# Experts' output layer on one Trainium2 core: the activations become the stationary operand

## What the reference computes

```python
h  = gelu(x_e @ W1[e] + b1[e])     # rows x 128 -> rows x 512
ye = h @ W2[e] + b2[e]             # rows x 512 -> rows x 128
out[rows of e] += gate * ye
```

## Time and profile before

| what | value |
|---|---|
| runs of the kernel | 1934.9, 1938.9, 1939.16 us; median 1938.9 us |
| profiled execution | 1937.17 us |
| its span | 1935.3 us |
| TensorE matmul busy | 1583.7 us (82%) |
| TensorE weight loads | 912.9 us (47%) |
| VectorE busy | 1304.5 us (67%) |
| GpSimd busy | 1071.9 us (55%) |
| ScalarE busy | 961.7 us (50%) |
| mean granted TensorE clock | 0.894 of full speed |

### The profile page before, as it was taken

One profiled execution on the slowest core, in us unless ns is written; L12 is line 12 of the kernel. 1 busy time (PEld: TensorE's weight loads), 2 busy tenths in 40 slices (PEclk: granted clock), 3 DMA queues, 4 the chain that ended last, 5 costly groups with the idle time before them and its releaser, 6 DMA issues. The chain is left out here.

```text
span 1935.3 us, 44569 instructions
## 1 busy us (share of the span) xinstructions
PE 1583.7 (82%) x16888; PEld 912.9 (47%) x16888; DVE 1304.5 (67%) x3246; ACT 961.7 (50%) x2039; POOL 1071.9 (55%) x1712
## 2 busy tenths in 40 slices
PE   5648878876499999985886699999999999958883
PEld 4522333345255555653443355565555565544341
DVE  7348888873678877875221788887888778773224
ACT  4215667742156667732232266777776777612221
POOL 3446666414377766404776476555666774206773
PEclk9966999977689999976998599999999999958986
DMA  7343323203433332202443442232332332104435
GB/s 233 92 122 96 93 69 95 80 24 106 120 107 111 91 91 86 71 23 71 101 110 80 135 125 77 93 93 86 93 93 83 100 99 82 41 26 94 103 97 164
DMA packets 224442, 181.81 MB, mean 94 GB/s; under 512 B 29702, under 2 KB 212454, under 8 KB 223846
## 3 DMA queue, kind: packets, MB, share of 16 engines
q1 hardware_dynamic: 213846, 157.97, 27.3%
q0 software_dynamic: 10240, 20.99, 5.0%
q10 hardware_dynamic: 144, 0.00, 0.0%
HBM read 104.34 MB, written 72.35 MB: 91 GB/s over the span
## 5 line engine op out<-in xcount | busy, mean ns | idle before, releaser
L900 DVE TENSOR_REDUCE mx<-PS 128x2 f32<-128x512 f32 (+3 forms) x1408 | 783.3, 611 | 202.5 <-PE PS L567 156.3
L750 ACT ACTIVATE pt<-PS 128x512 f32<-128x512 f32 (+2 forms) x1408 | 661.2, 537 | 273.8 <-PE PS L567 210.6
L583 PE MATMUL PS<-ka,qa 52*128 52x256 bf16 (+3 forms) x2048 | 477.7, 306 | 52.1 <-DVE mx L900 34.8
L692 PE MATMUL PS<-qa,ka 55*128 55x512 bf16 (+3 forms) x1792 | 459.7, 317 | 17.3 <-DMA qa<-nm 15.5
L637 PE MATMUL PS<-pt,vs 128*32 128x512 f32 (+3 forms) x3584 | 345.1, 478 | 0.7 <-ACT pt L750 0.7
L567 PE MATMUL PS<-mask_q,identh 64*128 64x64 bf16 x3072 | 312.3, 192 | 0.0
L567 PE MATMUL PS<-mask_k,identh 64*128 64x64 bf16 x3072 | 303.9, 189 | 0.0
L1394 POOL DMA_INDIRECT pt<-xn_rows,idx x160 | 155.4, 971 | 250.5 <-POOLq L553 155.6
L692 PEld LDWEIGHTS PS<-qa,ka 55*128 55x128 bf16 x1792 | 165.7, 93 | 247.0 <-issue 118.2
L567 PEld LDWEIGHTS PS<-mask_q,identh 64*128 64x128 bf16 x3072 | 255.9, 97 | 30.2 <-issue 5.6
L567 PEld LDWEIGHTS PS<-mask_k,identh 64*128 64x128 bf16 x3072 | 246.5, 95 | 47.4 <-issue 1.4
(11 more groups left out here) (242 smaller groups left out, 2332.4 us busy)
## 6 DMA issues: line engine op xcount, KB each, us to landing
pt<-in_f_w SPq DMA_DIRECT2D x96, 256.0 KB, 3.1
qa<-q_parts SPq DMA_DIRECT2D x256, 96.0 KB, 2.3
ka<-k_parts SPq DMA_DIRECT2D x192, 96.0 KB, 2.3
q_parts<-parts SPq DMA_DIRECT2D x32, 384.0 KB, 2.9
k_parts<-parts SPq DMA_DIRECT2D x24, 384.0 KB, 2.6
xn_rows<-xn SPq DMA_DIRECT2D x32, 256.0 KB, 2.9
xn<-y_rows SPq DMA_DIRECT2D x32, 256.0 KB, 3.4
hid<-y_rows SPq DMA_DIRECT2D x32, 256.0 KB, 4.4
```

Source lines behind the costliest of these rows:

```text
L583: mm = pe.matmul(PS[:, bank, i * n:(i + 1) * n], k.qa[rows, b % 2, g, h // 2, qb * P:(qb + 1) * P], k.ka[rows, b % 2, g, h // 2, 0:n], sta ...
L692: mm = pe.matmul(PS[:, bank, i * n:(i + 1) * n], k.ka[rows, b % 2, g, h // 2, kb * P:(kb + 1) * P], k.qa[rows, b % 2, g, h // 2, q0:S], st ...
L750: nc.scalar.activation(k.pt[:, u % 2, at[c]:at[c] + len(heads) * n], PS[:, SC_BANK + c % RING, 0:len(heads) * n], ACT.Exp, scale=SCORE_SCA ...
L900: nc.vector.tensor_reduce(out, PS[:, MX_BANK + t % RING, 0:len(heads) * n] .rearrange("p (h n) -> p h n", n=n), AX.X, ALU.max).then_inc(s. ...
```

## The change

TensorE computes the output layer with the two operands swapped. For each block f of hidden channels and each block t of 128 rows, `hT[:, par, f, t*P:(t+1)*P]` is the stationary operand and `w2[:, par, f, :]` (128 columns) moves. The product has the tokens on the partitions at once. So out_T, rows_back, the buffer `yT` and the semaphores `yT_full` and `yT_free` go; two PSUM banks (6 and 7) take the output layers of the experts in turn, and output(e) waits for result(e-2). The waits for the end of an output layer now use `y_full`.

```diff
-XT_BANK, H_BANK, YT_BANK, Y_BANK = 0, 2, 6, 7
+XT_BANK, H_BANK, Y_BANK = 0, 2, 6
@@ TensorE @@
             def output(e):
                 par = e % 2
                 pe.wait_ge(*s.w2_landed[par].at(16 * (e // 2 + 1)))
-                if e >= 1:
-                    pe.wait_ge(*s.yT_free.at(e))
+                if e >= 2:
+                    pe.wait_ge(*s.y_ready.at(e - 1))
                 for f in range(FC):
                     pe.wait_ge(*s.act_done.at(e * FC + f + 1))
-                    mm = pe.matmul(PS[:, YT_BANK, 0:capacity], k.w2[:, par, f, :], k.hT[:, par, f, 0:capacity],
-                                   start=(f == 0), stop=(f == FC - 1))
-                mm.then_inc(s.yT_full.h, 1)
-
-            def rows_back(e):
-                pe.wait_ge(*s.yT_free.at(e + 1))
-                if e >= 1:
-                    pe.wait_ge(*s.y_ready.at(e))
-                for t in range(ST):
-                    mm = pe.transpose(PS[:, Y_BANK, t * P:(t + 1) * P], k.yT[:, e % 2, t * P:(t + 1) * P], k.ident[:, :])
+                    for t in range(ST):
+                        mm = pe.matmul(PS[:, Y_BANK + par, t * P:(t + 1) * P], k.hT[:, par, f, t * P:(t + 1) * P],
+                                       k.w2[:, par, f, :], start=(f == 0 and t == 0), stop=(f == FC - 1 and t == ST - 1))
                 mm.then_inc(s.y_full.h, 1)
             for e in range(E):
                 hidden(e)
-                if e >= 1:
-                    rows_back(e - 1)
                 if e + 1 < E:
                     rows_T(e + 1)
                 output(e)
-            rows_back(E - 1)
@@ ScalarE @@
-                        act.wait_ge(*s.yT_full.at(e - 1))
+                        act.wait_ge(*s.y_full.at(e - 1))
@@ VectorE @@
-            def out_T(e):
-                dve.wait_ge(*s.yT_full.at(e + 1))
-                if e >= 2:
-                    dve.wait_ge(*s.y_full.at(e - 1))
-                nc.vector.tensor_copy(k.yT[:, e % 2, 0:capacity], PS[:, YT_BANK, 0:capacity]).then_inc(s.yT_free.h, 1)
             def result(e):
-                nc.vector.tensor_tensor(k.ys[ring][:, 0:ST, :], PS[:, Y_BANK, 0:capacity]
+                nc.vector.tensor_tensor(k.ys[ring][:, 0:ST, :], PS[:, Y_BANK + e % 2, 0:capacity]
                     result(e - 1)
                 if e + 1 < E:
                     rows(e + 1)
-                out_T(e)
                 if e == 0:
                     gates()
@@ SyncE @@
-                    sp.wait_ge(*s.yT_full.at(e - 1))
+                    sp.wait_ge(*s.y_full.at(e - 1))
```

More of the change, by code:

```diff
@@ L1433, in moe @@
         s.diff_ready: 2, s.exp_ready: 2, s.rt_step: k.route_steps, s.eT_full: E, s.eT_free: E,
-        s.h_full: FC * E, s.act_done: FC * E, s.yT_full: E, s.yT_free: E, s.y_full: E, s.y_ready: E,
+        s.h_full: FC * E, s.act_done: FC * E, s.y_full: E, s.y_ready: E,
     }
@@ L1502, in __init__ @@
         self.h_full, self.act_done = new("h_full"), new("act_done")
-        self.yT_full, self.yT_free = new("yT_full"), new("yT_free")
         self.y_full, self.y_ready = new("y_full"), new("y_ready")
@@ L1599, in program @@
         k.xe, k.ys = rows(5) + rows(9), rows(6) + [k.vst, k.ctx]
-        k.yT = k.qa[:, :, 0:2, :, :].rearrange("p b g s t -> p b (g s t)").bitcast(F32)
         k.xeT, k.w1 = part(7), part(8)
```

## The result

| | before | changed |
|---|---|---|
| median | 1936.9 us (4 runs) | 1915.61 us (4 runs: 1914.68 to 1917.91) |
| ratio | | 0.9894, 95% interval 0.9873 to 0.9914 |
| profiled execution | 1937.17 us | 1914.68 us |
| matmul records | 16888 | 17624 |
| TensorE busy, weight loads busy | 1583.7, 912.9 us | 1563.9, 969.8 us |

The time fell by 21 us, 1.1%. I predicted 1921 us within 1914 to 1930. Measured a second time beside other kernels the changed one took 1915.37 us, ratio 0.9911 (0.9892 to 0.9929).

A forecast was written before the change was run, and what follows sets the result against it. GpSimd's indirect DMAs were taken to bound the expert stages, so only its waits at their starts and ends count: 10.8 + 6.0 = 16.8 us off 1937.2 gives 1920.4, or 1922.1 from the median; forecast 1921 us, range 1914 to 1930.

The forecast's parts named there:

- What bounds the kernel: Expert stages: GpSimd's 10.20 us per large expert against TensorE's 7.8; only GpSimd's waits can be won, ceiling 32.4 us.
- TensorE's passes: Output layer: 32 passes at 0.111 us, 3.6 us for 3.87 per large expert; worth nothing in the middle of a stage.
- The rule that I named against the change: Loads overlap matmuls only where row groups differ: some 0.218 us a pass, 10.9 us of TensorE per large expert.
- Starts: First deliveries of the four expert stages come earlier as gates follow rows(1) at once: 2.4, 2.2, 3.1, 3.1, sum 10.8 us.
- Ends: Last deliveries of the four expert stages come earlier: 1.1, 1.1, 1.9, 1.9, sum 6.0 us, between 0 and 8.6.
- a bound of 7: VectorE's scalings stretching GpSimd's indirect DMA issues: at most 16 x 0.44 = 7 us to either side, taken as 0.
- Outside the stages: Everything between the four expert stages keeps its length.
- 1 (the ends don't gain): Starts gain, ends don't, as TensorE's clock is down to half there: gain about 11 us, 1927 us; chance 15%.
- 3 (no change): Stretched GpSimd issues and the ends eat the earlier start: no measurable change, 1932 to 1938 us; chance 7%.
- 2 (all waits go): Nearly all GpSimd waits go if gates take less and the clock rises earlier: 1907 to 1912 us; chance 5%.
- 4 (loads that don't hide): Output layer's loads don't hide behind passes: slower, about 1952 us at 0.222 a pass, 2050 at 0.30; chance 6%.
- twice the row: A pass of 0.222 us: 25 us lost on large experts, 6 us on small ones, less the 17 us gain, about 1952 us.

The follow-up runs named there:

- e8: The changed kernel with VectorE's 48 copies of a PSUM bank to the old buffer kept behind the bias addition: 1919.01 us, ratio 0.9937.
- e3: The changed kernel with the output layer's products of every second hidden block issued twice, 48 passes for 32 per large expert: 1930.16 us, ratio 0.9992.
- e9: The changed kernel with the gates held until output 0 is done, as the copy held them before: 1926.6 us, ratio 0.9961.
- e4: The changed kernel with every product of the output layer issued twice: 1988.3 us, ratio 1.0297.

## Why the prediction was right, point by point

- **What bounds the kernel**: right. GpSimd's cycle is 10.20 us before and after, and no gap appeared in mid-stage. e8 shows VectorE's copies free in the middle, e3 that half again as many passes cost 14.6 of 72 us. (TensorE's work for a large expert, 3.43 + 0.44 twice, sums to 7.7 us and not 7.8.)
- **TensorE's passes**: right, 0.112 us against 0.111 from line 663's row. The rule that I named against the change (the Trainium skill, "TensorE: Matmul & The Clock Gate", section "Part 3: Packing small matmuls — row/col tiling") doesn't hold for these shapes: 32 loads and their passes together took 3.57 us.
- **Starts**: 12.6 us against 10.8. The mechanism is shown by e9 (9.5 us back when the gates are held). The gates were late next, as forecast, in three stages. The surplus is luck: in the large stages I gave 3.1 each, and 3.6 and 4.1 came. In the fourth hidden 0 took 5.34 us where the same passes took 6.54 before, so rows(1) came 1.2 us earlier; in the third 5.33 in place of 5.81. Nothing in the change touches hidden 0. In the ten profiled executions without spare products it took from 5.20 to 6.73 us in a large stage, by when the granted clock rose. In the fourth stage the clock of the 5 us in question was 0.72 in place of 0.50 (hidden 0 and the window, of the changed kernel, then of before):

```profile
1731.44 5.34 PE L1248 MATMUL PS<-pt 128*128 128x512 f32 x8 [0.91 <-DVE pt L1341]
...
1732.00:1737.00 5.00, 5.00 (x12) 2.10 (x11) 0.54 (x2) 2.24 (x4) 3.78 (x5) 0.72 0.47 59
```

```profile
1746.14 6.54 PE L1248 MATMUL PS<-pt 128*128 128x512 f32 x8 [0.90 <-DVE pt L1350]
...
1746.70:1751.70 5.00, 5.00 (x7) 1.97 (x6) 0.54 (x2) 1.41 (x3) 3.78 (x5) 0.50 0.37 56
```

- **Ends**: 8.1 us against 6.0, the term that I sized too small. In the large stages I had TensorE's chain come 0.5 us after GpSimd; it came level (1038.55, no wait). GpSimd's 320 issues together took 1.65 us less (312.19 for 313.84), which I had left at 0 with a bound of 7. In the first stage 0.5 us came for 1.1: the last expert's rows were ready for the transposes 2.8 us after their fetch ended, 2.3 us before.
- **Outside the stages**: 0 forecast, 1.8 us measured (22.5 - 20.7). Nothing there was changed, and I have no experiment on it; single stretches between stages differ by 3 us both ways between kernels.
- **The rivals**: 1 (the ends don't gain) is out by the ends' 8.1 us, though the half clock that it feared was there: the output layer behind the long wait took 5.37 us in the changed third stage (5.78 before, 3.74 at the full clock). 3 (no change) is out by the 21 us. 2 (all waits go) came true in the large stages only, and there by the earlier clock; the gates took as long as before. 4 (loads that don't hide) is out by the load rows. But its threshold was wrong: I had a pass decide from 0.198 us, where e3, with as much of TensorE as passes of 0.167 us, already lost 14.6 us, mostly at the ends; and at twice the row I had 31 us of loss before the gains, where e4, which costs TensorE that much, lost 73.

## What to carry to other kernels

Find the engine that the others wait for in each stage; if it is in the middle of a stage another than the one whose work you cut, the gain is only in its waits at the stage's two ends, and these can be summed from the rows before anything is built. Ask what is queued on each engine between the event and the waiting engine: here nearly half of the gain was a copy that stood in front of an unrelated chain, and moving the chain gave the old kernel 8.6 us too. And an engine beside the bound has less room than the difference of the two cycles, since it must fill and drain in the same stage: in e3 it was 1.0 us per expert below the bound's cycle and still cost 14.6 us, because it sets the pace of the last experts.

## What the runs showed of the hardware that I had not expected

- What spare products on an idle TensorE give back isn't steady. In the two profiled executions of that kernel the first small stage started in 12.87 and 11.27 us (13.77 without them), the second in 11.04 and 13.03 us (14.03 without). In the two of these four that gave less (12.87 and 13.03) hidden 0 took 3.03 and 2.93 us in place of 1.99: the granted clock rose behind the spare passes, fell to 0.50 while hidden 0 ran and rose again. What decides it I haven't tried. Ahead of its first change, between 67 and 76 us in these executions, the profile's clock reads 1.00 and isn't to be relied on: in the changed kernel it reads 1.00 from 62 to 74 us, where hidden 0 of the first stage took 3.78 us, the pace of the half clock.
- The same kernel's runs differ by 0.6% (1926.6 to 1938.79 us for the kernel before, 25 runs on one chip), while a stage start read from the trace repeats within 0.3 us (20.45 and 20.60, 20.62 and 20.66 in two executions of the changed kernel); it moves with the length of hidden 0 too, by 1.0 and 1.2 us in e8's large stages. For effects of a few us the cut by stages told more than the medians.
